# A hand-written end for the last three batches and a reordered start in a cross-attention kernel

## The chip, the cores and the metric

One core of a Trainium2 chip. The time is device microseconds for one execution of the whole kernel, as the median of several runs; the trace comes from one profiled execution.

## The reference

Sixteen batches (B = 16) of cross attention, with 128 query tokens and 20 heads of 8 channels. The context of a batch has 124 text tokens and 4 image tokens of width 256. The image tokens have projections of their own, and their scores get half the cosine between the attended text and the image token.

```python
q = heads(hidden_states @ W_q)
k_t, v_t = heads(text_ehs @ W_k), heads(text_ehs @ W_v)
probs_t = softmax(q k_t^T * attn_scale)
text_out = probs_t v_t
k_ip, v_ip = heads(ip_ehs @ W_k_ip), heads(ip_ehs @ W_v_ip)
attn_scores = q k_ip^T * attn_scale
qsem = l2norm(probs_t @ text_ehs)
sem = qsem . l2norm(ip_ehs)
probs_ip = softmax(attn_scores + 0.5 * sem) * spatial_mask
out = (text_out + probs_ip v_ip) @ W_out + b_out + residual
```

## The kernel before

Each engine has a program written by hand, ordered by semaphores. All run the same loop of windows, one for each batch, w = -1 to 18: windows -1 to 3 and 14 to 18 are written out, 4 to 13 are a hardware loop of two. A window has five slots g = 0 to 4, one for each group of four heads (G = 5, HG = 4). `has(w, lag, ahead)` says whether window w has work for batch w - lag + ahead.

In the window of batch b, TensorE makes the scores of b's five groups (L706: `score_ps` from `q_stack` and `k_diag`, a block-diagonal K of four heads), turns the probs of the group two slots back (L723), and multiplies those of the group three slots back with `main_rhs` (L746, L748: V, the image columns and the Gram matrix of the context, for the value sums and the squared norm of `qsem`). Between these it prepares batch b + 1: the context's Gram matrix G, V and K into the bank `pa` (L686), Q into `pb` (L758), and the transposes of K and Q for groups 0 to 3 (L765, L775) and group 4 (L713, L714). It also finishes batch b - 3: the turn of `attn_out` (L695) and the output product (L732). A `pa` or `pb` product is K or Q split in two float32r parts, a high part copied by ScalarE (L448, L503) and a low part subtracted by VectorE (L633, L565).

ScalarE does the exponentials (L497), the copies `g_stage` (L444), `probsT` (L466) and `k_stack` (L485). It may overwrite `g_stage` only when its copy into `main_rhs`, ten times over, has landed (semaphore s_grep). VectorE does the row maxima (L628), the norms (L608, L610, called a group of norms below), the statistics `guard`, `rden`, `clamped` (L552 to L556) and small steps of the image softmax. GpSimd does the rest of that: a power for `rnorm` (L415, L429), `fused`, `centred`, `ip_probs`, `text`, and `ip_output` (L248 to L256), which weighs the image values (`vrep`) with `ip_probs`. In windows 16 to 18 `ip_output` is VectorE's.

SyncE issues every DMA, in the order of its program. In a window: `k_split` rows of the image tokens from `kip_d`, the context and x of batch b + 2, later xn and `vrep`, then four copies `k_stack` to `k_diag` (L314), `main_rhs` from `g_stage` (L319), four more `k_diag` copies (L324), and the output of b - 3. `kip_d` and `vip_d` are DRAM tensors that the prologue writes with the image projections of all batches. The scores of batch b + 1 wait for its `k_diag` copies (s_kd03, s_kd4), the transposes of K for it wait for its `k_split` load (s_kip_in).

## Time and profile before

| what | us |
|---|---|
| median of 3 runs (lowest, highest) | 233.81 (233.21, 235.36) |
| the profiled execution, its own time | 234.08 |
| its span, first to last instruction | 232.0 |
| TensorE, matmul busy | 207.8 (90% of the span) |
| VectorE busy | 190.8 (82%) |
| ScalarE busy | 170.0 (73%) |
| GpSimd busy | 154.4 (67%) |

Busy shares are means over stages with different limits. Mean granted TensorE clock: 0.958 of full speed. In the profile PE is TensorE, DVE VectorE, ACT ScalarE, POOL GpSimd and SPq the queue of SyncE, which issues the DMAs. A float32 matmul shows as two passes, so a product over two halves of a contraction is x4.

### The profile page before, as it was taken

The numbers are of one execution on the slowest core, as the hardware profiler recorded it, in microseconds if no ns is written. First come the engines' busy times: TensorE is split into PE (matmuls) and PEld (weight loads), VectorE is DVE, ScalarE is ACT, GpSimd is POOL, SyncE is SP. The second block draws the span as 40 slices with busy tenths as digits, with TensorE's granted clock in tenths as the row PEclk, the third lists the DMA queues.
The fourth block names the chain that finished last, engine by engine and source line by source line (L and its number), as shares of the span: only waits on it lengthen the run. The fifth ranks groups of instructions, "written<-read, shape, count | busy, mean of one in ns | idle before, by whom it ended". The sixth has DMA issues, their size and how long they took to land.

```text
span 232.0 us, 6889 instructions
## 1 busy us (share of the span) xinstructions
PE 207.8 (90%) x1562; PEld 192.6 (83%) x1562; DVE 190.8 (82%) x1149; ACT 170.0 (73%) x561; POOL 154.4 (67%) x263
## 2 busy tenths in 40 slices
PE   1948989999999999999999999999999999988433
PEld 1647879998898999999999999999999999977222
DVE  5753778796979798998979897989798979998862
ACT  2063978897978798897969797988888888975000
POOL 5611003649596868788796969696969696979650
PEclk9976999999999999999999999999999999999955
DMA  5405433465355545373736353646454553533030
GB/s 150 124 18 154 104 101 66 124 172 142 104 160 143 149 132 163 87 206 82 204 80 186 104 172 99 167 119 158 132 152 144 145 149 106 143 87 85 1 100 14
DMA packets 46348, 28.57 MB, mean 123 GB/s; under 512 B 7897, under 2 KB 43898, under 8 KB 46330
## 3 DMA queue, kind: packets, MB, share of 16 engines
q1 hardware_dynamic: 46330, 28.38, 44.6%
q8 instruction: 6, 0.10, 0.2%
q14 instruction: 12, 0.10, 0.1%
HBM read 11.11 MB, written 1.52 MB: 54 GB/s over the span
## 4 chain that ended last, share of the span: by engine, by line
PE 61%; DMA 9%; DVE 8%; POOL 7%; ACT 6%; issue 4%; SPq 3%; DVEq 0%; POOLq 0%; ACTq 0%
PE main_ps L746 11%; PE main_ps L748 11%; PE probsT_ps L723 10%; PE pa L686 9%; DMA main_rhs<-g_stage 6%; PE score_ps L706 6%; PE pb L732 5%; POOL rnorm L429 3%; PE pb L758 3%; PE pa L765 2%; ACT probs L497 2%; DVE junk L608 2%; PE pa L775 2%; SPq L324 1%; PE pb L695 1%
## 5 line engine op out<-in xcount | busy, mean ns | idle before, releaser
L497 ACT ACTIVATE probs<-score_ps,negmax 128x124 f32<-128x124 f32 x320 | 93.3, 413 | 0.7 <-DVE negmax L628 0.6
L608 DVE CUSTOM_DVE_ANT_0 junk<-main_ps,probs 128x124 f32<-128x124 f32 x320 | 78.0, 281 | 2.3 <-PE main_ps L748 1.5
L746 PE MATMUL main_ps<-main_rhs,probsT 124*128 124x137 f32 x320 | 65.1, 284 | 1.5 <-DVE small L610 1.4
L748 PE MATMUL main_ps<-main_rhs,probsT 124*128 124x137 f32 x320 | 63.3, 279 | 0.0
L429 POOL TENSOR_TENSOR rnorm<-clamped,exponent 128x20 f32<-128x20 f32 (+1 forms) x16 | 54.8, 3427 | 1.1 <-DVE clamped L556 1.1
L628 DVE TENSOR_REDUCE negmax<-score_ps 128x4 f32<-128x496 f32 x80 | 53.1, 664 | 0.0
L466 ACT ACTIVATE probsT<-probsT_ps 124x512 f32<-124x512 f32 x80 | 51.1, 639 | 2.8 <-PE probsT_ps L723 2.0
L746 PEld LDWEIGHTS main_ps<-main_rhs,probsT 124*128 124x128 f32 x320 | 48.9, 190 | 3.5 <-issue 2.6
L748 PEld LDWEIGHTS main_ps<-main_rhs,probsT 124*128 124x128 f32 x320 | 48.7, 188 | 0.0
L723 PE MATMUL probsT_ps<-ident_sb,probs 128*124 128x128 f32 x320 | 48.2, 273 | 0.0
L723 PEld LDWEIGHTS probsT_ps<-ident_sb,probs 128*124 128x124 f32 x320 | 38.4, 139 | 5.2
L706 PE MATMUL score_ps<-k_diag,q_stack 128*128 128x512 f32 x80 | 39.0, 488 | 0.3 <-ACT probs L497 0.3
L627 DVE COPY ip_score<-score_ps 128x16 f32<-128x16 f32 x80 | 13.3, 166 | 21.4 <-PE score_ps L706 21.4
L610 DVE COPY small<-main_ps 128x26 f32<-128x26 f32 x160 | 28.8, 180 | 0.0
L608 DVE DVE_READ_ACCUMULATOR2_ANT norm<- 128x1 f32 x320 | 26.6, 83 | 0.2 <-issue 0.2
L444 ACT ACTIVATE g_stage<-pa 128x128 f32<-128x128 f32 x16 | 4.4, 278 | 26.5 <-PE pa L686 16.4
L686 PE MATMUL pa<-wkv_sb,ctxT_sb 128*128 128x160 f32 x128 | 21.9, 319 | 0.0
L399 POOL TENSOR_TENSOR ip_exp_half<-ip_exp 128x40 f32<-128x40 f32 x16 | 4.0, 253 | 25.7 <-ACT ip_exp L491 25.7
L686 PEld LDWEIGHTS pa<-wkv_sb,ctxT_sb 128*128 128x128 f32 x128 | 19.8, 208 | 0.0
L248 POOL TENSOR_TENSOR ip_prod<-vrep,ip_probs 128x640 f32<-128x640 f32 x13 | 18.3, 1404 | 0.0
L409 POOL TENSOR_TENSOR main_rhs<-v_stage,one 124x80 f32<-124x80 f32 x16 | 5.1, 321 | 18.9 <-PE main_ps L748 8.9
L732 PE MATMUL pb<-wout_sb,oT 96*128 96x160 f32 x64 | 14.2, 349 | 2.9 <-DVE oT L620 2.9
(91 smaller groups left out, 339.2 us busy)
## 6 DMA issues: line engine op xcount, KB each, us to landing
main_rhs<-g_stage SPq DMA_DIRECT2D x16, 660.0 KB, 4.1
vrep<-vip_d SPq DMA_DIRECT2D x16, 320.0 KB, 3.5
k_diag<-k_stack SPq DMA_DIRECT2D x60, 64.0 KB, 2.1
ctxT_sb<-ctxT SPq DMA_DIRECT2D x16, 124.0 KB, 2.6
xT_sb<-xT SPq DMA_DIRECT2D x16, 80.0 KB, 2.0
xn_sb<-xn SPq DMA_DIRECT2D x16, 80.0 KB, 2.0
out<-out_sb SPq DMA_DIRECT2D x16, 80.0 KB, 1.7
k_diag<-k_stack SPq DMA_DIRECT2D x60, 16.0 KB, 2.0
```

The costliest lines, as they stand in the source:

```text
L429: pool.tensor_tensor(rnorm[:, heads], clamped[:, heads], exponent[:, heads], ALU.pow).then_inc(s_rnorm, 1)
L466: act.activation(probsT[tp][:, :, :].rearrange("t h s -> t (h s)"), probsT_ps[tp][0:T, :], ACT.Copy).then_inc(s_probsT, 1)
L497: last = act.activation(probs[p][:, h, :], score_ps[(p * G + g) % 2][:, j * TOK:j * TOK + T], ACT.Exp, bias=negmax[p][:, h:h + 1])
L608: dve.tensor_tensor_reduce(junk[:, 2 * r + a, :], u, probs[wb][:, h, :], 1.0, 0.0, ALU.mult, ALU.add, norm2[wb][:, h:h + 1])
L610: dve.tensor_copy(small[wb][:, PG * gg + r, :], main_ps[r][:, T:T + SMALL]).then_inc(s_norm, 1)
L628: dve.tensor_reduce(negmax[p][:, HG * g:HG * g + HG], sc[:, :, 0:T], AX_X, ALU.max, negate=True).then_inc(s_max, 1)
L686: mm = pe.matmul(pa[:, lo:lo + width], ctxT_sb[n][:, c, :], r, start=(c == 0), stop=(c == EC - 1))
L706: pe.matmul(score_ps[(p * G + g) % 2][:, :], q_stack[p][:, g, :], k_diag[p][:, g, :, :].rearrange("r h t -> r (h t)"), start=True, stop=Tr ...
L723: mm = pe.transpose(probsT_ps[tp][0:T, j * S:(j + 1) * S], probs[tb][:, HG * tg + j, :], ident_sb[:, :])
L732: mm = pe.matmul(pb[:, 0:C], oT[:, c, :], wout_sb[:, c, :], start=(c == 0), stop=(c == 1))
L746: pe.matmul(main_ps[r][:, 0:MAIN], probsT[mp][:, 2 * r, :], blk[:, RW - MAIN:RW], start=True, stop=True)
L748: pe.matmul(main_ps[r][:, MAIN:2 * MAIN], probsT[mp][:, 2 * r + 1, :], blk[:, 0:MAIN], start=True, stop=True).then_inc(s_main, 1)
```

## The change

The windows are now 0 to 15. What was window -1 is written out at the head of each engine's program, and what were windows 16 to 18 at the end.

At the start, the loads go out in the order of need, those of K and Wq from ScalarE's queue. TensorE first does ten products on a zero tile. K of batch 0 and of batch 1 gets its four image rows from a product with `zip_sb`, a tile that is zero but for the image tokens' columns, accumulated into the same bank. The Gram matrix of batch 0 comes after the transposes and the image products; the first score follows, and then batch 1's K, V and G. Wq is scaled by ScalarE. The copies `kip_split`, `vip_sb` and the new `vipT_sb` are made by VectorE in window 0, slot 2, and `kip_d`, `vip_d`, `smask`, `wout` and the new `hmask` are moved by SyncE after `main_rhs0` and before window 0's own DMAs. The memset of `k_diag1` on GpSimd comes after V of batch 0 is in `main_rhs0`.

At the end, the last three batches (13, 14, 15) do without `vrep` and `ip_output`. For each a small matrix `vw_sb` = blockdiag(V_ip) W_out is made (`vspread`, L1077), and the output is the sum of two products, one from the turned text part and one from the turned image probs. Statistics and powers of batch 15 go in three parts of 12, 4 and 4 heads (`PARTED`). Its text, fused scores, centring and masking are VectorE's. The tiles of this part are its own.

Tiles of 96 rows become 80 or 81. The middle windows are the same.

```diff
-PARTED = 3
+PARTED = (0, 3, 4, 5)
+TAIL = 3
+LAST = B - TAIL
...
+            sp.dma_start(ctxT_sb[0][:, :, 0:T], ctxT[0]).then_inc(s_ctx_in[0], 16)
+            sp.wait_ge(s_zip, 1)
+            sp.dma_start(zip_sb[0][:, :, T:TOK], ipT[:, :, 0:NIP]).then_inc(s_zip_in[0], 16)
+            sp.dma_start(xT_sb[0][:, :, :], xT[0]).then_inc(s_xT_in[0], 16)
+            sp.dma_start(ident_sb[:, :], ident).then_inc(s_ident_in, 16)
             sp.dma_start(ip_sb[:, :], ipn).then_inc(s_ipn_in, 16)
-            sp.dma_start(ipT_sb[:, :, :], ipT).then_inc(s_ipw_in, 16)
-            sp.dma_start(wkvip_sb[:, :, :], wkvip).then_inc(s_ipw_in, 16)
...
-            sp.dma_start(wkv_sb[:, :, :], wkv).then_inc(s_wkv_in, 16)
-            sp.dma_start(ctxT_sb[0][:, :, 0:T], ctxT[0]).then_inc(s_ctx_in[0], 16)
-            sp.wait_ge(s_fill, 1)
-            sp.dma_start(wq_sb[0:CH, :, :], wq).then_inc(s_wq_in, 16)
...
+            sp.dma_start(wkv_sb[:, :, 0:C], wkv[:, :, 0:C]).then_inc(s_wv_in, 16)
+            sp.dma_start(ipT_sb[:, :, :], ipT).then_inc(s_ipT_in, 16)
+            sp.dma_start(wkvip_sb[:, :, C:2 * C], wkvip[:, :, C:2 * C]).then_inc(s_wvip_in, 16)
             sp.dma_start(ctxT_sb[1][:, :, 0:T], ctxT[1]).then_inc(s_ctx_in[1], 16)
...
+            sp.wait_ge(s_zip, 3)
+            sp.dma_start(zip_sb[1][:, :, T:TOK], ipT[:, :, NIP:2 * NIP]).then_inc(s_zip_in[1], 16)
+            sp.dma_start(xT_sb[1][:, :, :], xT[1]).then_inc(s_xT_in[1], 16)
+            sp.wait_ge(s_gstage, 1)
+            sp.dma_start(main_rhs[0][:, :, D + 1:D + 1 + NIP + TOK],
+                         g_stage[:, :].unsqueeze(1).broadcast_to([TOK, NPAIR, NIP + TOK])).then_inc(s_grep[0], 16)
             sp.wait_ge(s_kip, 2)
-            sp.dma_start(k_split[T:TOK, :, :, :, :].rearrange("t h c a d -> t (h c a d)").bitcast(F32),
-                         kip_split[0:NIP, :, :, :, :].rearrange("t h c a d -> t (h c a d)")).then_inc(s_kip_in, 16)
             sp.dma_start(kip_d, kip_split[:, :, :, :, :].rearrange("t h c a d -> t (h c a d)")).then_inc(s_kip_out, 16)
...
             sp.dma_start(vip_d, vip_sb[:, :]).then_inc(s_vip_out, 16)
             sp.dma_start(smask_sb[:, :], smask).then_inc(s_const_in, 16)
-            sp.dma_start(wout_sb[0:CH + 1, :, :], wout).then_inc(s_const_in, 16)
-            sp.wait_ge(s_fill, 3)
...
-            sp.wait_ge(s_vip_out, 16)
...
+            pool.wait_ge(s_k0_mm, 1)
+            pool.tensor_copy(ctxT_sb[0][:, :, T:TOK], ipunitT[:, :, 0:NIP]).then_inc(s_ipcol, 1)
+            pool.wait_ge(s_v0, 1)
+            v_columns(0)
             pool.memset(k_diag[1][:, :, :, :].bitcast(F32), 0.0).then_inc(s_zeros[1], 1)
-            pool.wait_ge(s_fill, 3)
...
+            for k in range(3):
+                heads = slice(HG * PARTED[k], HG * PARTED[k + 1])
+                pool.wait_ge(s_tail_stats, 3 * (k + 1))
+                pool.tensor_tensor(tail_rnorm[:, heads], tail_clamped[:, heads], exponent[:, heads],
+                                   ALU.pow).then_inc(s_tail_rnorm, 1)
...
+            act.dma_start(wkv_sb[:, :, C:2 * C], wkv[:, :, C:2 * C]).then_inc(s_wk_in, 16)
+            act.dma_start(wkvip_sb[:, :, 0:C], wkvip[:, :, 0:C]).then_inc(s_wkip_in, 16)
+            act.dma_start(wq_sb[:, :, :], wq).then_inc(s_wq_in, 16)
+            act.wait_ge(s_wq_in, 16)
+            act.activation(wq_scaled[:, :, :], wq_sb[:, :, :], ACT.Copy, scale=SCALE).then_inc(s_wq, 1)
+            act.wait_ge(s_k0_mm, 1)
+            act.activation(k_split[:, :, :, 0, :], doubled(probsT_ps[0][:, 0:C]), ACT.Copy).then_inc(s_khi, 1)
+            act.wait_ge(s_q_mm, 1)
+            act.activation(q_split[:, :, 0, :, :], doubled(probsT_ps[1][:, 0:C]), ACT.Copy).then_inc(s_qhi, 1)
...
+            act.wait_ge(s_qlo, 1)
+            act.activation(v_stage[:, :], probsT_ps[1][0:T, C:2 * C], ACT.Copy).then_inc(s_v0, 1)
+            act.wait_ge(s_ctx_mm, 1)
+            act.activation(g_stage[:, NIP:NIP + TOK], pa[:, 0:TOK], ACT.Copy)
+            act.activation(g_stage[:, 0:NIP], pa[:, T:TOK], ACT.Copy).then_inc(s_gstage, 1)
...
+                    if g == 2 and w == 0:
+                        dve.wait_ge(s_vipT_mm, 1)
+                        kips = doubled(main_ps[0][0:B * NIP, 0:C])
+                        dve.tensor_copy(kip_split[:, :, :, 0, :].bitcast(F32R), kips).then_inc(s_kip, 1)
+                        dve.wait_ge(s_kip, 1)
+                        dve.tensor_tensor(kip_split[:, :, :, 1, :].bitcast(F32R), kips, kip_split[:, :, :, 0, :],
+                                          ALU.subtract).then_inc(s_kip, 1)
+                        dve.tensor_copy(vip_sb[:, :], main_ps[0][0:B * NIP, C:2 * C]).then_inc(s_vip, 1)
+                        dve.tensor_copy(vipT_sb[:, :, :, :].rearrange("p x k m -> p (x k m)"),
+                                        main_ps[0][0:CH, 2 * C:2 * C + 2 * TAIL * NIP]).then_inc(s_vipT, 1)
                     if has_group(w, g, 4):
...
+            norms(B, 0, 0)
+            norms(B, 0, 1)
...
+            stats(1, PARTED[0], PARTED[1], tiles, s_tail_stats, 0)
+            norms(B, 0, 2)
...
+            stats(1, PARTED[1], PARTED[2], tiles, s_tail_stats, 3)
+            dve.wait_ge(s_fuse, 2 * (B - 1))
+            dve.tensor_reduce(ipmax[:, :], fused[:, :, :], AX_X, ALU.max).then_inc(s_ipmax, 1)
+            dve.wait_ge(s_ipmax, B - 1)
+            dve.tensor_tensor(tail_centred[0][:, :, :], fused[:, :, :],
+                              ipmax[:, :].unsqueeze(2).broadcast_to([S, H, NIP]), ALU.subtract).then_inc(s_tail_centred, 1)
+            norms(B, 0, 3)
...
+            stats(1, PARTED[2], PARTED[3], tiles, s_tail_stats, 6)
...
+            text_out(0, text[0], rden)
+            dve.wait_ge(s_tail_stats, 9)
+            text_out(1, tail_text, tail_rden)
...
+            pe.wait_ge(s_warm, 1)
+            for k in range(10):
+                pe.matmul(main_ps[1][:, 0:128], warm[:, :], warm[:, :], start=True, stop=True)
+            pe.wait_ge(s_ctx_in[0], 16)
+            pe.wait_ge(s_zip, 2)
+            pe.wait_ge(s_wk_in, 16)
+            project(probsT_ps[0][:, 0:C], ctxT_sb[0], lambda c: wkv_sb[:, c, C:2 * C], True, False)
+            pe.wait_ge(s_zip_in[0], 16)
+            pe.wait_ge(s_wkip_in, 16)
...
+            pe.wait_ge(s_ipcol, 1)
+            pe.wait_ge(s_kst03, 1)
+            pe.wait_ge(s_kd03[0], 64)
+            project(pa[:, 0:TOK], ctxT_sb[0], lambda c: ctxT_sb[0][:, c, :], True, True).then_inc(s_ctx_mm, 1)
...
+                    if g == 0 and w == 0:
+                        pe.wait_ge(s_ctx_in[1], 16)
+                        pe.wait_ge(s_gstage, 1)
...
+                        project(pa[:, TOK + C:TOK + 2 * C], ctxT_sb[1], lambda c: wkv_sb[:, c, C:2 * C], True, False)
+                        pe.wait_ge(s_zip_in[1], 16)
+                        project(pa[:, TOK + C:TOK + 2 * C], zip_sb[1], lambda c: wkvip_sb[:, c, 0:C], False, True)
+                        project(pa[:, TOK:TOK + C], ctxT_sb[1], lambda c: wkv_sb[:, c, 0:C], True, True).then_inc(s_k1_mm, 1)
+                        pe.wait_ge(s_ipcol, 2)
+                        project(pa[:, 0:TOK], ctxT_sb[1], lambda c: ctxT_sb[1][:, c, :], True, True).then_inc(s_ctx_mm, 1)
...
+            def turn_text(src, bank):
+                for x in range(2):
+                    mm = pe.transpose(bank[0:CH, x * S:(x + 1) * S], src[:, x * CH:(x + 1) * CH], ident_sb[:, :])
+                return mm
+            def turn_probs(src, bank):
+                return pe.transpose(bank[0:H * NIP, 2 * S:3 * S], src[:, :, :].rearrange("s h m -> s (h m)"), ident_sb[:, :])
+            def project_text(k, bank):
+                for x in range(2):
+                    pe.matmul(bank[:, 0:C], tailT[k][:, x, :], wout_sb[:, x, :], start=(x == 0), stop=False)
+            def project_probs(k, bank):
+                return pe.matmul(bank[:, 0:C], tailT[k][0:H * NIP, 2, :], vw_sb[:, k, :], start=False, stop=True)
...
+            for k in range(TAIL):
+                pe.wait_ge(s_vspread, k + 1)
+                for x in range(2):
+                    mm = pe.matmul(pb[0:CH, k * C:(k + 1) * C], vspread[:, k, x, :], wout_sb[0:CH, x, :],
+                                   start=(x == 0), stop=(x == 1))
+            mm.then_inc(s_vw_mm, 1)
...
+            pe.wait_ge(s_tail_text, 1)
+            turn_text(text[0], score_ps[0]).then_inc(s_tail_tr, 1)
+            pe.wait_ge(s_tail_text, 2)
+            turn_text(tail_text, score_ps[1]).then_inc(s_tail_tr, 1)
+            pe.wait_ge(s_tail_T, 1)
+            project_text(0, pa)
+            pe.wait_ge(s_vw, 1)
+            project_probs(0, pa).then_inc(s_tail_mm, 1)
+            pe.wait_ge(s_tail_T, 2)
+            pe.wait_ge(s_tail_probs, 1)
+            turn_probs(tail_probs[0], score_ps[0]).then_inc(s_tail_tr, 1)
+            pe.wait_ge(s_probsT, B * G)
+            project_text(1, probsT_ps[0])
+            pe.wait_ge(s_tail_T, 3)
+            project_text(2, probsT_ps[1])
+            pe.wait_ge(s_tail_T, 4)
+            project_probs(1, probsT_ps[0]).then_inc(s_tail_mm, 1)
+            pe.wait_ge(s_tail_probs, 2)
+            turn_probs(tail_probs[1], score_ps[1]).then_inc(s_tail_tr, 1)
+            pe.wait_ge(s_tail_T, 5)
+            project_probs(2, probsT_ps[1]).then_inc(s_tail_mm, 1)
```

SyncE, from the last constant of the prologue to window 1's first DMA, before; 0 and 1 in the names are the buffers of even and odd batches, `k_diag1` is batch 1's.

```order
L280 DMA wout_sb<-wout 81x320
L319 DMA main_rhs0<-g_stage 128x10x132 [waits s_zeros1,s_kst03,s_vip_out,s_gstage,s_kip_out,s_fill]
L292 DMA k_split<-kip_d 4x640 [waits s_kq4,s_kT,s_st4]
L297 DMA ctxT_sb0<-ctxT 128x2x124 [waits s_ctx_mm]
L299 DMA xT_sb0<-xT 80x256 [waits s_q_mm]
L314 DMA k_diag1<-k_stack 32x4x128 [waits s_kst03]
L314 DMA k_diag1<-k_stack 32x4x128 x3
L319 DMA main_rhs1<-g_stage 128x10x132 [waits s_gstage]
L324 DMA k_diag1<-k_stack 32x128 [waits s_st4]
L324 DMA k_diag1<-k_stack 32x128 x3
L292 DMA k_split<-kip_d 4x640 [waits s_kq4,s_kT]
```

The same place in the changed program, up to the first `k_diag1` copy of group 4.

```order
L329 DMA main_rhs0<-g_stage 128x10x132 [waits s_gstage]
L332 DMA kip_d<-kip_split 64x640 [waits s_kip]
L334 DMA vip_d<-vip_sb 64x160 [waits s_vip]
L335 DMA smask_sb<-smask 128x1
L336 DMA wout_sb<-wout 81x320
L337 DMA hmask_sb<-hmask 80x40
L353 DMA ctxT_sb0<-ctxT 128x2x124 [waits s_ctx_mm,s_zeros1]
L355 DMA xT_sb0<-xT 80x256 [waits s_q_mm]
L373 DMA k_diag1<-k_stack 32x4x128 [waits s_kst03]
L373 DMA k_diag1<-k_stack 32x4x128 x3
L378 DMA main_rhs1<-g_stage 128x10x132 [waits s_gstage]
L383 DMA k_diag1<-k_stack 32x128 [waits s_st4]
```

`main_rhs0` goes ahead of five DMAs that stood before it, and these now stand ahead of window 0's loads and `k_diag1` copies.

TensorE, from the last Q transposes of batch 0 to the score product of group 1, before.

```order
L775 MATMUL main_ps1<-ident_r_sb,q_split 128x128 x3
L713 MATMUL pb<-ident_r_sb,k_split 128x128 [waits s_qlo]
L714 MATMUL pb<-ident_r_sb,q_split 128x128
L686 MATMUL pa<-ctxT_sb1 128x128 [waits s_kst03,s_qst03,s_ipcol,s_ctx_in1]
L686 MATMUL pa<-ctxT_sb1 128x128
L686 MATMUL pa<-wkv_sb,ctxT_sb1 128x160 x4
L706 MATMUL score_ps0<-k_diag0,q_stack0 128x512 [waits s_qst03,s_kd030,s_kst03]
L758 MATMUL pb<-wq_scaled,xT_sb1 128x160 [waits s_st4,s_xT_in1]
L758 MATMUL pb<-wq_scaled,xT_sb1 128x160
L706 MATMUL score_ps1<-k_diag0,q_stack0 128x512
```

TensorE in the changed program, from the end of the image products to batch 1's Q.

```order
L906 MATMUL main_ps0<-ipT_sb,wkvip_sb 80x12 x4
L865 MATMUL pa<-ctxT_sb0 128x128 [waits s_kd030,s_kst03,s_ipcol]
L865 MATMUL pa<-ctxT_sb0 128x128
L984 MATMUL score_ps0<-k_diag0,q_stack0 128x512 [waits s_kd030,s_qst03,s_ipunitT,s_kst03]
L865 MATMUL pa<-wkv_sb,ctxT_sb1 128x160 [waits s_zip,s_gstage,s_ctx_in1]
L865 MATMUL pa<-wkv_sb,ctxT_sb1 128x160
L865 MATMUL pa<-wkvip_sb,zip_sb1 128x160 [waits s_zip_in1]
L865 MATMUL pa<-wkvip_sb,zip_sb1 128x160
L865 MATMUL pa<-wkv_sb,ctxT_sb1 128x160 x2
L865 MATMUL pa<-ctxT_sb1 128x128 [waits s_ipcol]
L865 MATMUL pa<-ctxT_sb1 128x128
L1024 MATMUL pb<-wq_scaled,xT_sb1 128x160 [waits s_st4,s_xT_in1,s_kd40]
```

The first score stands ahead of batch 1's products instead of behind them; the Gram matrix of batch 0 and two products with `zip_sb1` have joined the row.

VectorE, the last ten instructions before, for batches 14 and 15.

```order
L615 TENSOR_REDUCE ipmax<-fused 128x20 [waits s_fuse]
L620 COPY oT<-pb 80x256 [waits s_final_mm,s_oT_tr]
L582 RECIPROCAL rip<-ipsum 128x20 [waits s_ipprobs,s_ipsum]
L594 TENSOR_TENSOR out_sb0<-pb,xn_sb0 128x160 [waits s_store0,s_xn_in0,s_final_mm]
L248 TENSOR_TENSOR ip_prod<-vrep1,ip_probs 128x640 [waits s_ipout,s_ipprobs,s_vrep_in1]
L253 TENSOR_TENSOR ip_half<-ip_prod 128x320 [waits s_ipout]
L256 TENSOR_TENSOR ip_out<-ip_half 128x160 [waits s_attn,s_ipout]
L577 TENSOR_TENSOR attn_out<-ip_out,text1 128x160 [waits s_oT_tr,s_text,s_ipout]
L620 COPY oT<-pb 80x256 [waits s_final_mm,s_oT_tr]
L594 TENSOR_TENSOR out_sb1<-pb,xn_sb1 128x160 [waits s_store1,s_xn_in1,s_final_mm]
```

VectorE in the changed program, the last but one twelve, from the image softmax of batch 14 to its output.

```order
L800 TENSOR_REDUCE tail_sum<-tail_exp0 128x20 [waits s_tail_exp,s_const_in]
L802 RECIPROCAL tail_rip<-tail_sum 128x20 [waits s_tail_chain]
L804 SCALAR_TENSOR_TENSOR tail_probs0<-tail_exp0,smask_sb,tail_rip 128x80 [waits s_tail_chain]
L833 TENSOR_TENSOR tail_fused<-small1,tail_rnorm 128x80 [waits s_tail_rnorm]
L836 TENSOR_TENSOR tail_fused<-tail_fused,ip_score1 128x80 [waits s_fuse]
L838 TENSOR_REDUCE tail_max<-tail_fused 128x20 [waits s_fuse]
L840 TENSOR_TENSOR tail_centred1<-tail_fused,tail_max 128x80 [waits s_ipmax]
L845 TENSOR_TENSOR out_sb1<-pa,xn_sb1 128x160 [waits s_store1,s_xn_in1,s_tail_mm]
L800 TENSOR_REDUCE tail_sum<-tail_exp1 128x20 [waits s_tail_exp]
L802 RECIPROCAL tail_rip<-tail_sum 128x20 [waits s_tail_chain]
L804 SCALAR_TENSOR_TENSOR tail_probs1<-tail_exp1,smask_sb,tail_rip 128x80 [waits s_tail_chain]
L850 TENSOR_TENSOR out_sb0<-probsT_ps0,xn_sb0 128x160 [waits s_store0,s_xn_in0,s_tail_mm]
```

The rounds of `ip_prod`, `ip_half`, `ip_out`, `attn_out` and `oT` are gone; both batches' image softmaxes follow each other, and only the outputs are left behind them.

## Rows read from the trace of the kernel before

**Rows 1.** Timeline of TensorE, score products of group 0, windows 0, 1, 3, 4, 6, 14. Columns: start us, us, engine, line, operation, output and inputs, count.
```profile
19.64 0.83 PE L706 MATMUL score_ps<-k_diag,q_stack 128*128 128x512 f32 x1
...
29.77 0.50 PE L706 MATMUL score_ps<-k_diag,q_stack 128*128 128x512 f32 x1
...
54.16 0.50 PE L706 MATMUL score_ps<-k_diag,q_stack 128*128 128x512 f32 x1
...
67.29 0.50 PE L706 MATMUL score_ps<-k_diag,q_stack 128*128 128x512 f32 x1
...
92.50 0.50 PE L706 MATMUL score_ps<-k_diag,q_stack 128*128 128x512 f32 x1
...
189.04 0.50 PE L706 MATMUL score_ps<-k_diag,q_stack 128*128 128x512 f32 x1
```

**Rows 2.** The chain of waits at the start: start us, us, what.
```profile
16.25 4.67 DMA main_rhs<-g_stage
...
32.19 2.75 DMA k_split<-kip_d
```

**Rows 3.** Timeline of SyncE's queue, and TensorE's K transposes of window 1; brackets: idle before.
```profile
8.93 0.58 SPq L276 DMA_DIRECT2D kip_d<-kip_split  x1
...
23.77 2.70 SPq L314 DMA_DIRECT2D k_diag<-k_stack  x4
26.51 0.66 SPq L319 DMA_DIRECT2D main_rhs<-g_stage  x1
28.63 3.47 SPq L324 DMA_DIRECT2D k_diag<-k_stack  x4
...
35.07 0.64 PE L765 MATMUL pa<-ident_r_sb,k_split 128*128 128x128 f32 x4 [1.09 <-DMA k_split<-kip_d]
```

**Rows 4.** The chain of waits at the end: the last output product and its addition.
```profile
228.07 1.45 PE pb L732 x4
229.55 0.33 DVE out_sb L594
```

**Rows 5.** Timeline of VectorE: the cast in the prologue, and Q's low part in window 0.
```profile
8.38 2.96 DVE L534 CAST ident_r_sb<-ident_sb 128x128 fp32r<-128x128 f32 x1
...
23.24 0.49 DVE L565 TENSOR_TENSOR q_split<-pb,q_split 128x320 fp32r<-128x320 f32 x1 [0.19 <-ACT q_split L503]
```

**Rows 6.** The chain of waits: the twelve passes of G, V and K, prologue and steady windows.
```profile
8.36 3.07 PE pa L686 x12
...
103.33 1.53 PE pa L686 x12
```

**Rows 7.** DMA issues of the first 22 us: KB each, median us to landing.
```profile
wq_sb<-wq SPq DMA_DIRECT2D x1, 100.0 KB, 4.6
```

**Rows 8.** ScalarE's groups, 5 to 20 us, by form: busy us, mean ns, idle before.
```profile
L479 ACT ACTIVATE k_diag<-pa 32x512 fp32r<-32x512 f32 x4 | 2.4, 588 | 0.9 <-PE pa L765 0.8
```

**Rows 9.** Timeline of ScalarE in window 1.
```profile
30.70 0.28 ACT L444 ACTIVATE g_stage<-pa 128x128 f32<-128x128 f32 x1 [0.58 <-DMA main_rhs<-g_stage]
...
35.74 0.60 ACT L485 ACTIVATE k_stack<-pa 128x512 f32<-128x512 f32 x1 [1.86 <-PE pa L765]
```

**Rows 10.** Timeline of VectorE behind the last scores.
```profile
211.79 0.29 DVE L608 CUSTOM_DVE_ANT_0 junk<-main_ps,probs 128x124 f32<-128x124 f32 x1 [0.49 <-PE main_ps L748]
...
213.46 0.22 DVE L552 SCALAR_TENSOR_TENSOR guard<-small 128x12 f32<-128x12 f32 x1 [0.25 <-POOL text L379]
...
217.11 0.28 DVE L608 CUSTOM_DVE_ANT_0 junk<-main_ps,probs 128x124 f32<-128x124 f32 x1
...
218.12 0.41 DVE L620 COPY oT<-pb 80x256 f32<-80x256 f32 x1
```

**Rows 11.** Timeline of GpSimd: the two parts of batch 15's power.
```profile
214.82 2.28 POOL L415 TENSOR_TENSOR rnorm<-clamped,exponent 128x12 f32<-128x12 f32 x1
...
219.39 1.64 POOL L429 TENSOR_TENSOR rnorm<-clamped,exponent 128x8 f32<-128x8 f32 x1
```

**Rows 12.** Windows view, the last 12 us: busy us by engine, granted clock, DMA share, GB/s.
```profile
220.00:232.00 12.00, 4.17 (x12) 2.49 (x12) 5.64 (x14) 0.27 (x1) 3.62 (x9) 0.50 0.21 55
```

557 lines of the change are left out of this document (372 added, 185 removed).

## Prediction

> **What bounds the kernel now.** I read the page first, then the starts of the score products, then the chain of waits at both ends. The score product of group 0 opens each batch's window; its starts [rows 1] cut the run in three: 19.64 us of prologue, windows 1 to 5 at (92.50 - 29.77)/5 = 12.55 us, and windows 6 to 13 at (189.04 - 92.50)/8 = 12.07 us with TensorE in every piece of the chain. That last number is the work of TensorE; the change leaves it alone, so only the two ends can move the time.
>
> At the start the chain is not TensorE's. It runs through the copy of g_stage into main_rhs0 (issued 16.25, landed 20.92), on which ScalarE waits before it may take batch 1's projection and then the first probs, and later through a small k_split load issued only at 32.19, landed 34.94, which releases the K transposes of window 1 at 35.07 [rows 2, 3]. From 35.07 to 50 the chain is TensorE without a gap. So the question for the prologue is not when the first score starts but **when that product at 35.07 starts**. Why the load is issued so late is seen in SyncE's own queue [rows 3]: four k_diag copies from 23.77 to 26.47, main_rhs1 at 26.51, four more k_diag copies from 28.63 that take 3.47 us.
>
> At the end the last score is done at about 209, and from there to 232.0 one engine after another waits for VectorE's and GpSimd's short steps; each of the last batches costs a whole round through VectorE, TensorE, VectorE, TensorE, VectorE, the last one ending 229.55 + 0.33 [rows 4].
>
> **The start, walked through.** Three things are taken away. The 2.96 us cast of ident_r_sb and the scaling of wq beside it, which were stretched while GpSimd cleared k_diag1 [rows 5]: the cast now comes when GpSimd is idle and the scaling is ScalarE's. The image K copy into k_split becomes part of a product. And main_rhs0 no longer waits for kip_d, vip_d and two constants to be written. Against this stand ten warm products and a longer chain of its own. TensorE's speed here is known at two levels: twelve passes took 3.07 us at 8.36 and 1.53 us at 103.33 [rows 6], so 0.256 or 0.128 us a pass. The warm products are 20 passes from about 1.6 (VectorE's first memset): done at 4.2 to 6.7. K0 is 8 passes: slow, done at 8.7; fast, it is the wq load that holds ScalarE (issued about 2.0, landing 4.6 after its issue [rows 7], then the scaling 0.4: 7.0). Copy and subtraction of the split are 0.5 each, and the Q and V products 1.0: the K transposes start at 8.0 to 9.7; I take 8.7. Then transposes 0.7, two k_diag copies on each of two engines at 0.59 each [rows 8] instead of four on one, group 4's copies, the unit image rows, the image products (8 long and 8 short passes, about 1.5), the G product 0.5 and g_stage 0.45, with a hand-over of 0.05 to 0.1 between engines: 5.2 us in all, so main_rhs0 is issued at **13.9**, 2.35 earlier than 16.25. Bounds: 13.2, and 16.2 if TensorE runs at the slow rate all through. First score about 13.8, nearly 6 us before 19.64.
>
> Now what it brings. ScalarE gets past g_stage at 13.9 + 4.67 = 18.6 instead of 20.92. But kip_d now needs two VectorE copies placed in window 0 behind the first three waits on ScalarE (k_split, then probs of group 0, then q_split; the subtraction behind them ended at 23.7, 2.8 us after the landing) and these take 0.5 each (0.49 for the same form of subtraction) [rows 5]: SyncE stands at that wait until 18.6 + 2.8 + 2 x 0.5 = 22.4. Behind it in the same queue stand kip_d, vip_d, smask, wout, hmask, ctxT and xT, seven issues at 0.58 (kip_d's row [rows 3]), 4.1 us, and only then the k_diag copies of window 1: 26.4 instead of 23.77, **2.6 later**. main_rhs1 moves by the same, to 29.1; in the run before, the second four k_diag copies had 1.46 us of slack behind it (27.17 to 28.63), so they and the k_split load behind them start 2.6 - 1.4 = 1.2 later. ScalarE comes to the same: g_stage of window 1 waits for main_rhs1 (30.70 before), now 33.3, and had 1.86 us idle before k_stack [rows 9]; 0.7 to 1.1 late. So the earlier first score is handed back in the queue, and window 1's K transposes start **1.2 us later**, at about 36.3. With main_rhs0 at 13.2 this is 0.5, with 16.2 it is 3.5. On the gain side it is bounded too: TensorE stood idle only 1.09 us before the product at 35.07 [rows 3], so a load landing early gives at most that. VectorE's four new copies in window 0 (1.5 us) delay probs of group 2 by 0.9; ScalarE has that slack, and the queue above is later anyway. GpSimd's memsets and three spreads in window 0 lie in an idle stretch (it does nothing there that window 1 waits for).
>
> The Trainium skill, page DMA: Bandwidth & Descriptors, section Issuing engines are not separate DMA queues, says that transfers started from two engines run on the same 16 DMA engines and that a second issuer saves only issue time. By that rule the second queue is worth three issues, some 1.5 to 2 us of the first loads, and nothing of their landing once the engines are full; no run here shows it yet, and since my walk hangs on the slow products and on the queue in window 0, it leaves the sum as it is.
>
> **The tail, walked through.** Up to the norms of batch 15's group 2, at 211.79 + 1.0 = 212.8, both programs are the same but for three transposes on TensorE, 0.15 us. A group of norms takes 1.01 us (217.11 to 218.12), a short operation 0.22 (the row at 213.46) [rows 10]; three statistics in a row overlap, and I give them 0.4. VectorE after 212.9: statistics 0.4, norms 1.0, statistics and two short ones 0.9, norms 1.0, statistics 0.4, two text products at 0.33: 217.3. GpSimd's powers run beside it, 2.28 for 12 heads and 1.64 for 8 [rows 11], so 0.16 a head and about 1.0 for four: done at 217.6, hidden. Then three short ones for batch 14 (0.7), four for batch 15 (0.9) and an exponential 0.3, out_sb 0.33 beside it, three short ones (0.7), a transpose, ScalarE's copy and one product (1.1), out_sb 0.33, and hand-overs of 0.05 to 0.1, some 14 of them, 0.9: **222.2** where it was 229.88, and 2.1 more to the end of the store, 224.3. What goes: ip_prod, ip_half, ip_out and attn_out three times, and the strictly serial rounds.
> The price unknown is TensorE's clock. The granted clock is 0.50 over the last 12 us before [rows 12], and there one output product took 1.45 us [rows 4]. If it is at half from 217 on, the two late text products (8 passes at 0.256), three image products and the transposes set the end instead of VectorE, about 2.2 us later: 226.5. There is more TensorE work now between 214 and 217 (12 passes for vw), which speaks for the full rate at first; I take 225.0, near the fast end because VectorE's chain is serial and sets it either way until 220. Tail: **7.0 us shorter**, 5.5 to 7.7.
>
> **Sum.** The profiled execution is 234.08 us with a span of 232.0. Span 232.0 + 1.2 - 7.0 = 226.2, execution 228.3; the median of the runs is 0.27 below the profiled one, so 228.0.
>
> **Rivals.** (a) *The queue does not bind.* The k_diag copies' lateness is covered, and window 1's K transposes move up by the 1.1 us that TensorE allows: 233.8 - 1.1 - 7.0 = 225.7; all 2.35 us of the earlier main_rhs0 carried on: 224.5. For it: the four k_diag issues ahead of that load took 3.47 us where the four before took 2.70 [rows 3], so some of the queue's time is waiting for room, which may fall otherwise now; against it: seven issues in order have no way round. (b) *Half clock in the tail*: 4.8 us gained there, 230.2. (c) *A slow prologue*, main_rhs0 at 16.2: 233.8 + 3.5 - 7.0 = 230.3. (d) *Slower than before: the queue never catches up.* Windows 1 to 5 cost 12.55 instead of 12.07 because main_rhs lands late for g_stage. If the later start in the queue keeps this going at the 1.06 us that window 3 lost (54.16 to 67.29 is 13.13 [rows 1]) through the nine windows to 14, it costs 9.5 us: 233.8 + 1.2 + 9.5 - 7.0 = 237.5. It decides from 0.65 us a window. Against it: windows 6 to 13 are free of it, and the TensorE work that ends them is unchanged. (e) *The change does not do what it says*: first score no sooner than 18; that is (c) at its worst.
>
> **How the numbers follow.** Forecast 0.52; (a) 0.20, of it 0.05 at 224.5; (b) 0.13; (c) with (e) 0.11; (d) and the like 0.04. The range leaves out the far ends of (a), and (d): 224.8 to 231.0. Within 1% (2.3 us either way, about what runs of this kernel can tell from no change) needs both a slow prologue and a half-clock tail: 0.09; faster 0.87; slower 0.04.
>
> **What would show it.** Right: first score near 13.8; SyncE idle until about 22, the first k_diag copy of window 1 near 26, the K transposes of window 1 at 35.5 to 37; windows from 6 on at 12.07; last out_sb 13 us or so after the last score where it was 21. Wrong: k_diag copies issued before 24, K transposes of window 1 before 34, windows that differ from 12.07, or a tail in which TensorE, not VectorE, fills the chain.

## The result, and the profile after

The changed kernel takes 225.66 us (median of 4 runs, 225.16 to 226.25), the kernel before on the same chip 234.24 us (4 runs, 233.21 to 235.36): ratio 0.963, 95% interval 0.958 to 0.969. The profiled span is 223.5 us where it was 232.0, the mean granted clock of TensorE 0.992 where it was 0.958.

I read the starts of the score products first, as before [rows 1]: timeline of TensorE, group 0 of windows 0, 1, 3, 4, 6 and 14.

```profile
12.22 0.47 PE L984 MATMUL score_ps<-k_diag,q_stack 128*128 128x512 f32 x1
...
29.00 0.50 PE L984 MATMUL score_ps<-k_diag,q_stack 128*128 128x512 f32 x1 [0.97 <-DMA k_diag<-k_stack]
...
53.97 0.50 PE L984 MATMUL score_ps<-k_diag,q_stack 128*128 128x512 f32 x1
...
67.11 0.50 PE L984 MATMUL score_ps<-k_diag,q_stack 128*128 128x512 f32 x1
...
91.32 0.50 PE L984 MATMUL score_ps<-k_diag,q_stack 128*128 128x512 f32 x1
...
188.40 0.50 PE L984 MATMUL score_ps<-k_diag,q_stack 128*128 128x512 f32 x1
```

The first score comes 7.4 us sooner (12.22 for 19.64), window 1 only 0.8, windows 3 and 4 0.2, window 6 1.2, and all behind it 0.6. Windows 6 to 13 take (188.40 - 91.32)/8 = 12.13 us, before 12.07; the difference is all in window 6, which takes 12.64 us (its neighbours 12.10 and 12.04). What happened to the 7.4 us stands in SyncE's queue and beside it on ScalarE, which answer to [rows 3, 9]: timeline of SyncE, then TensorE's K transposes of window 1; below them ScalarE. The copy of `g_stage` into `main_rhs` is called the ring copy from here on.

```profile
12.87 0.65 SPq L329 DMA_DIRECT2D main_rhs<-g_stage  x1
20.76 0.57 SPq L332 DMA_DIRECT2D kip_d<-kip_split  x1
...
24.83 2.69 SPq L373 DMA_DIRECT2D k_diag<-k_stack  x4
27.57 0.67 SPq L378 DMA_DIRECT2D main_rhs<-g_stage  x1
28.28 3.41 SPq L383 DMA_DIRECT2D k_diag<-k_stack  x4
31.81 0.41 SPq L348 DMA_DIRECT2D k_split<-kip_d  x1
...
34.84 0.65 PE L1031 MATMUL pa<-ident_r_sb,k_split 128*128 128x128 f32 x4
```

```profile
17.09 0.28 ACT L576 ACTIVATE g_stage<-pa 128x128 f32<-128x128 f32 x1 [4.25 <-DMA main_rhs<-g_stage]
...
31.80 0.28 ACT L576 ACTIVATE g_stage<-pa 128x128 f32<-128x128 f32 x1 [5.08 <-DMA main_rhs<-g_stage]
```

The first ring copy goes out at 12.87 instead of 16.25. ScalarE waits 4.25 us for it, since there is one g_stage; VectorE's copies of the image rows (`kip_split`, `vip_sb`, `vipT_sb`) come behind that; SyncE stands until 20.76, works without a gap from there, sends the second ring copy at 27.57 (26.51 before), and ScalarE waits 5.08 us for that one too. The K transposes of window 1 start at 34.84, before at 35.07: 3.4 us are down to 0.2.

The end answers to [rows 4, 11, 12]. The last score product, before and then changed:

```profile
208.56 0.49 PE L706 MATMUL score_ps<-k_diag,q_stack 128*128 128x512 f32 x1
```

```profile
207.91 0.49 PE L984 MATMUL score_ps<-k_diag,q_stack 128*128 128x512 f32 x1
```

Then, from the changed kernel, the timeline of GpSimd's last power, the chain of waits behind it (start us, us, engine, output, line), and the windows view of the last stretches (stretch, its length, busy us of PE, weight loads, DVE, ACT and POOL, then the granted clock, the DMA share and GB/s).

```profile
216.38 1.02 POOL L525 TENSOR_TENSOR tail_rnorm<-tail_clamped,exponent 128x4 f32<-128x4 f32 x1 [0.35 <-DVE tail_clamped L698]
```

```profile
217.57 0.16 DVE tail_fused L833
...
218.30 0.25 DVE tail_centred L840
...
218.58 0.28 ACT tail_exp L644
...
219.46 0.31 DVE tail_probs L804
...
219.82 0.32 PE score_ps L1053
...
220.16 0.28 ACT tailT L625
...
220.49 0.55 PE probsT_ps L1062 x2
...
221.07 0.33 DVE tail_out L853
```

```profile
216.00:220.00 4.00, 3.62 (x26) 2.94 (x24) 3.65 (x17) 1.71 (x5) 1.05 (x2) 1.00 0.06 20
220.00:223.50 3.50, 0.67 (x3) 0.30 (x2) 0.33 (x1) 0.27 (x1) 0.00 (x0) 1.00 0.15 47
```

### The profile page after: what moved, and what is told of

Same layout as the page of the kernel before. It is cut to its first block, busy times and chain, and to the rows that moved or that the text cites. A ratio compares the mean times of both kernels' runs of the same rounds, so it can differ in the third digit from the quotient of the medians.

```text
span 223.5 us, 6984 instructions
## 1 busy us (share of the span) xinstructions
PE 210.6 (94%) x1619; PEld 197.6 (88%) x1619; DVE 183.7 (82%) x1147; ACT 172.7 (77%) x569; POOL 149.3 (67%) x255
## 4 chain that ended last, share of the span: by engine, by line
PE 68%; DVE 9%; DMA 8%; POOL 4%; issue 4%; ACT 3%; SPq 3%; DVEq 0%; POOLq 0%; ACTq 0%
PE main_ps L952 13%; PE main_ps L954 12%; PE probsT_ps L934 11%; DMA main_rhs<-g_stage 8%; PE pa L924 8%; PE score_ps L984 6%; PE pb L1012 4%; DVE junk L713 3%; PE pb L1024 3%; PE pa L1031 2%; PE main_ps L870 2%; PE pa L1039 2%; POOL rnorm L500 2%; SPq L373 1%; PE probsT_ps L865 1%
## 5 line engine op out<-in xcount | busy, mean ns | idle before, releaser
L500 POOL TENSOR_TENSOR rnorm<-clamped,exponent 128x20 f32<-128x20 f32 x15 | 53.2, 3544 | 1.2 <-DVE clamped L698 1.2
L934 PE MATMUL probsT_ps<-ident_sb,probs 128*124 128x128 f32 x320 | 49.0, 276 | 0.0
L934 PEld LDWEIGHTS probsT_ps<-ident_sb,probs 128*124 128x124 f32 x320 | 39.1, 141 | 5.3 <-issue 0.4
L478 POOL TENSOR_TENSOR ip_exp_half<-ip_exp 128x40 f32<-128x40 f32 x14 | 3.5, 252 | 25.1 <-ACT ip_exp L606 25.1
L576 ACT ACTIVATE g_stage<-pa 128x128 f32<-128x128 f32 x15 | 4.2, 278 | 20.5 <-DMA main_rhs<-g_stage 13.5
L924 PE MATMUL pa<-wkv_sb,ctxT_sb 128*128 128x160 f32 x112 | 17.5, 299 | 0.0
L984 PEld LDWEIGHTS score_ps<-k_diag,q_stack 128*128 128x128 f32 x80 | 15.4, 193 | 1.2 <-DMA k_diag<-k_stack 1.2
L600 ACT ACTIVATE k_stack<-pa 128x512 f32<-128x512 f32 x15 | 9.0, 598 | 9.4 <-PE pa L1031 9.3
L924 PEld LDWEIGHTS pa<-wkv_sb,ctxT_sb 128*128 128x128 f32 x112 | 15.7, 190 | 0.0
```

Source lines behind the costliest of these rows:

```text
L500: pool.tensor_tensor(rnorm[:, :], clamped[:, :], exponent[:, :], ALU.pow).then_inc(s_rnorm, 1)
L924: mm = pe.matmul(pa[:, lo:lo + width], ctxT_sb[n][:, c, :], r, start=(c == 0), stop=(c == EC - 1))
L934: mm = pe.transpose(probsT_ps[tp][0:T, j * S:(j + 1) * S], probs[tb][:, HG * tg + j, :], ident_sb[:, :])
L984: pe.matmul(score_ps[(p * G + g) % 2][:, :], q_stack[p][:, g, :], k_diag[p][:, g, :, :].rearrange("r h t -> r (h t)"), start=True, stop=Tr ...
```

## The experiments

Times are medians. The experiments ran in three sets, each on a chip of its own: old_tail, kip_early, consts_first and no_warm (the kernel before took 234.34 us there); gs2, kip_gs2, kip_fill and one_part (234.42); gs2_consts, after_fill, kip_gs2_fill and best2 (234.63).
**The new prologue alone** (old_tail). The tail's code of all engines is taken back:

```diff
-            for w in range(B - 2, B):
+            for w in range(B - 2, B + 3):
...
-            norms(B, 0, 0)
-            norms(B, 0, 1)
...
```

> The new prologue with the tail of the kernel before (windows B to B+2 for every engine, statistics in two parts, image output on VectorE, no vspread, no vw). Theory, the start's gain is handed back in window 0 and only the tail saves: start and middle as in the changed kernel (last group's scores at 207.9, 0.65 us ahead of the kernel before), tail as before (21.3 us from the last score to the end instead of 13.5), so 225.7 + 7.8 = 233.5 us, 0.7 below the kernel before (0.997). Rival, the prologue alone is worth the 3.4 us by which its first ring copy is issued earlier, and the written-out tail hides that: 230.8 us (0.985). Second rival, the 0.65 us in the middle is of the tail's code in window 0 or of chance: 234.2 us (1.000).

Measured: 234.63 us, ratio 1.002, interval 0.998 to 1.006 (10 runs). That is 1.1 above the theory's 233.5 and nearest to the second rival's 234.2. The prologue alone is worth nothing that can be measured; the tail is worth 234.63 - 225.66 = 9.0 us by the medians.
```profile
36.00:38.00 2.00, 2.00 (x10) 1.84 (x10) 1.51 (x12) 1.97 (x7) 0.00 (x0) 0.50 0.00 1
...
220.00:234.00 14.00, 5.45 (x16) 3.37 (x16) 6.61 (x20) 0.27 (x1) 4.89 (x11) 0.51 0.16 47
```

**The image row copies earlier** (kip_early).

```diff
-                    if g == 2 and w == 0:
+                    if g == 0 and w == 0:
                         dve.wait_ge(s_vipT_mm, 1)
                         kips = doubled(main_ps[0][0:B * NIP, 0:C])
...
```

(The block also stands behind the first scores' maxima now, ahead of the wait for ScalarE's k_split.)

> The changed kernel with VectorE's four copies of the image rows (kip_split in two passes, vip_sb, vipT_sb) made between its first two uses of the scores, at group 0 of window 0, instead of at group 2, so that they run at about 13.5 to 15 us, in VectorE's idle 4.4 us, and SyncE's kip_d, vip_d, three constants, ctxT and xT are issued by about 18.5 instead of 24.8. Theory, SyncE's queue in window 0 hands the start's gain back: the k_diag copies of window 1 at 20 to 20.5 (k_stack is ready at 19.97), its ring copy main_rhs at 22.8 to 23.2 instead of 27.57, its K transposes at 30.5 to 32.5 instead of 35.09, and 221.4 to 223.2 us in all, 2.5 to 4.3 below the changed kernel (225.66). Rival, another chain of window 1 (the projections, GpSimd's v columns, the clock of TensorE) is just as late: transposes at 34 to 35, 225.0 to 225.7 us.

Measured: 222.68 us, 3.0 below the changed kernel, transposes at 32.39: the theory. The gain stands at the transposes (2.45 us) and grows little behind them (2.62 at the last score). SyncE's timeline:

```profile
14.86 0.56 SPq L332 DMA_DIRECT2D kip_d<-kip_split  x1
...
20.71 2.97 SPq L373 DMA_DIRECT2D k_diag<-k_stack  x4
23.73 0.68 SPq L378 DMA_DIRECT2D main_rhs<-g_stage  x1
```

SyncE now waits for k_stack (ScalarE ends it at 20.69), not the other way round.

**Only the constants earlier** (consts_first).

```diff
             sp.dma_start(xT_sb[1][:, :, :], xT[1]).then_inc(s_xT_in[1], 16)
+            sp.dma_start(smask_sb[:, :], smask).then_inc(s_const_in, 16)
+            sp.dma_start(wout_sb[:, :, :], wout).then_inc(s_const_in, 16)
+            sp.dma_start(hmask_sb[:, :, :], hmask).then_inc(s_hmask_in, 16)
```

(The same three lines are gone from behind `vip_d`.)

> The changed kernel with three SyncE DMAs alone moved: smask, wout and hmask are issued right behind xT of batch 1, while SyncE has nothing to do, instead of behind vip_d; they took 22.02 to 23.54 us there. Theory, SyncE's queue in window 0 is the path: everything behind them 1.3 to 1.5 us earlier (k_diag copies of window 1 at 23.4, main_rhs at 26.1), 224.2 to 224.4 us. Rival, the queue is not the path: 225.7 us. A loss would come only from the three loads delaying wvip, ctxT or main_rhs of window 0 in the DMA rings: up to 1 us later first ring copy, 225.7 to 226.7.

```profile
30.00:32.00 2.00, 0.66 (x5) 0.36 (x3) 0.76 (x4) 1.66 (x7) 0.00 (x0) 1.00 0.10 26
32.00:34.00 2.00, 1.55 (x8) 1.58 (x9) 2.00 (x14) 1.52 (x5) 0.00 (x0) 0.66 0.45 109
34.00:36.00 2.00, 2.00 (x10) 1.82 (x10) 1.23 (x12) 0.79 (x3) 0.00 (x0) 0.50 0.00 0
```

My rival here (the queue is not the path, 225.7) came nearer in time than the theory and is wrong by the rows. The 226.48 also lies in the range that I gave for a loss, but its reason, a later first ring copy, did not happen (12.90 for 12.87). The 0.5 us by which the profiled execution ends behind the changed kernel's come in window 6 (13.24 us for 12.64, see gs2 below). The four runs have mean clocks of 0.984 to 0.988, those of the changed kernel 0.983 to 0.992.

**Two g_stage buffers** (gs2).

```diff
-        g_stage = sb("g_stage", [TOK, NIP + TOK])
+        g_stage = two(sb, "g_stage", [TOK, NIP + TOK])
...
-                        wait(act, s_grep[p], 16 * (i + 1))
+                        wait(act, s_grep[n], 16 * (i + p))
```

> The changed kernel with two g_stage buffers instead of one (ScalarE writes g_stage[n] for batch b+1 and waits only for the ring copy of batch b-1 out of it), nothing else. In the changed kernel ScalarE stands idle 4.25 us at 12.85 to 17.09 and 5.08 us before 31.80, both times for main_rhs's copy out of the one g_stage. [...] Rival, SyncE's queue alone is the path, and it is full by itself: 225.0 to 225.7. A loss is possible only if the k_split copies sooner delay the first probs: below 0.5 us.

Measured: 222.01 us, 3.7 below the changed kernel. ScalarE takes batch 1's projection as soon as TensorE has it; kip_d goes out at 19.62 (a microsecond later than I expected, with probs and q_split of window 0 still ahead of it), the transposes start at 32.60, and the clock is 1.00 throughout:

```profile
15.95 0.28 ACT L576 ACTIVATE g_stage<-pa 128x128 f32<-128x128 f32 x1 [3.02 <-PE pa L865]
```

Only 2.2 us of the 3.7 are there at the transposes. The other 1.5 come in later windows, where the one g_stage costs too. ScalarE in the changed kernel, windows 3 and 6:

```profile
55.32 0.28 ACT L576 ACTIVATE g_stage<-pa 128x128 f32<-128x128 f32 x1 [1.29 <-DMA main_rhs<-g_stage]
...
92.24 0.28 ACT L576 ACTIVATE g_stage<-pa 128x128 f32<-128x128 f32 x1 [1.38 <-DMA main_rhs<-g_stage]
```

These windows take 13.14 and 12.64 us there; in gs2, where ScalarE no longer waits for a ring copy, 12.20 and 12.11. The kernel before has the same waits in windows 3, 4 and 5 (1.29, 1.24 and 1.37 us; the windows 13.13, 12.52 and 12.69).

**Both** (kip_gs2: the two diffs together).

> Both together: VectorE's four image row copies at group 0 of window 0 (kip_early, measured 222.68) and two g_stage buffers. [...] Rival, with kip_early done the g_stage wait has slack of its own and only the clock spell moves: 221.5 to 222.7. From 211 us of TensorE work no less than 216 is to be had.

Measured: 219.15 us, transposes at 31.00. The single gains are 2.98 and 3.65, together 6.51: nearly the sum, as it must be where two waits lie behind each other on one path; that the second g_stage also shortens later windows adds to it. Runs at 218.2 and 218.3 (mean clock 0.996, 0.999) and at 220.0 and 220.2 (0.992).

**The constants again, behind two buffers** (gs2_consts).

> gs2 with smask, wout and hmask issued behind xT of batch 1. By itself that move brought SyncE's queue forward by 1.43 us (k_diag copies at 23.41) and no time (226.48), because window 1 took 14.88 us instead of 13.29, with TensorE at 1.2 GHz from 33 to 36 us behind an idle 1.8 us in which ScalarE stood at the ring copy out of the one g_stage. Theory, the queue is the path and what took the gain was that wait with the clock behind it: with two g_stage buffers the 1.4 us come through, k_diag copies of window 1 at 22.2 to 22.4 instead of 23.68, 220.5 to 221.0 us. Rival, the three constants are not on the path at all: 221.7 to 222.3 us.

Measured: 221.33 us, 0.7 below gs2, between theory and rival (runs 220.53 to 222.11; gs2 is of another set, 221.70 to 222.27). In its profile the k_diag copies start at 22.54 and the transposes at 31.57, 1.1 and 1.0 sooner than in gs2, though the prologue of this execution was 0.3 later. So most of the queue's gain comes through once ScalarE's wait is gone; by the times alone this would be weak.

**Without the warm products** (no_warm).

```diff
-            pe.wait_ge(s_warm, 1)
-            for k in range(10):
-                pe.matmul(main_ps[1][:, 0:128], warm[:, :], warm[:, :], start=True, stop=True)
```

> [...]
Measured: 231.07 us, 5.4 above the changed kernel, where I expected 0.7 to 1.7 at the most. TensorE, changed kernel first, then no_warm:

```profile
1.06 4.49 PE L870 MATMUL main_ps<-warm 128*128 128x128 f32 x20 [1.06 <-DVE warm L651]
5.39 0.71 PE L865 MATMUL probsT_ps<-wkv_sb,ctxT_sb 128*128 128x160 f32 x4
```

```profile
4.04 1.44 PE L865 MATMUL probsT_ps<-wkv_sb,ctxT_sb 128*128 128x160 f32 x4 [4.04 <-DMA ctxT_sb<-ctxT]
...
16.42 0.77 PE L981 MATMUL score_ps<-k_diag,q_stack 128*128 128x512 f32 x1
...
19.51 1.27 PE L865 MATMUL pa<-wkv_sb,ctxT_sb 128*128 128x160 f32 x4
21.10 0.71 PE L865 MATMUL pa<-ctxT_sb 128*128 128x128 f32 x4 [0.31 <-POOL ctxT_sb L435]
```

The warm products do not only make the first K product fast; they even start it 1.35 us later (5.39 for 4.04). Without them the groups of four take 1.27 instead of 0.71 us until 21 us, the whole prologue: first ring copy at 17.17, transposes at 39.97. That the granted clock shows 1.00 in these stretches is no help; the duration of one shape is the better witness.

**Filling the idle time of TensorE in window 0** (kip_fill and after_fill: the same edit on kip_early and on the changed kernel; kip_gs2_fill: six products on kip_gs2).

```diff
+                    if g == 1 and w == 0:
+                        for k in range(12):
+                            pe.matmul(main_ps[1][:, 0:128], warm[:, :], warm[:, :], start=True, stop=True)
                     if g == 1 and has(w, ahead=1):
                         wait(pe, s_klo, b + 2)
```

> [...]
The loss in after_fill I did not expect: its windows 2 and 3 took 25.9 us together instead of 24.8. ScalarE waited 1.30 and 1.86 us there for the ring copy out of the one g_stage, 0.76 and 1.29 in the changed kernel, 1.1 us in sum. One_part, whose program is the changed kernel's up to the tail, has such a wait of 1.65 in window 2 (12.57 us for 11.68). So this wait differs between executions without any fill, and whether the twelve products have a part in it stays open.

My account of kip_gs2's two pairs falls: kip_gs2_fill has runs at 218.4 to 218.8 and at 219.7 and 219.9, with the clock at 0.998 or more in all. Its profiled run, 219.88, shows another tie: image row loads that land late in windows 3 and 4, which take 12.79 and 13.13 us instead of 12.12 in kip_gs2. The second stands on SyncE behind the store of a result whose issue takes 1.77 us, 0.58 in kip_gs2; the first is issued at 50.31, behind four k_diag copies. TensorE, then SyncE ahead of the second:

```profile
52.37 0.63 PE L1034 MATMUL pa<-ident_r_sb,k_split 128*128 128x128 f32 x4 [0.45 <-DMA k_split<-kip_d]
...
65.56 0.66 PE L1034 MATMUL pa<-ident_r_sb,k_split 128*128 128x128 f32 x4 [0.83 <-DMA k_split<-kip_d]
```

```profile
61.19 1.77 SPq L388 DMA_DIRECT2D out<-out_sb  x1
63.40 0.30 SPq L348 DMA_DIRECT2D k_split<-kip_d  x1
```

**Statistics of the tail in one part** (one_part).

```diff
-            for k in range(3):
-                heads = slice(HG * PARTED[k], HG * PARTED[k + 1])
-                pool.wait_ge(s_tail_stats, 3 * (k + 1))
-                pool.tensor_tensor(tail_rnorm[:, heads], tail_clamped[:, heads], exponent[:, heads],
-                                   ALU.pow).then_inc(s_tail_rnorm, 1)
+            pool.wait_ge(s_tail_stats, 3)
+            pool.tensor_tensor(tail_rnorm[:, :], tail_clamped[:, :], exponent[:, :], ALU.pow).then_inc(s_tail_rnorm, 1)
```

(VectorE's statistics, in one part too, are not shown.)

> The changed kernel with batch 15's statistics and power in one part of 20 heads behind the last norms instead of three parts of 12, 4 and 4 heads: VectorE runs six short statistics fewer (0.8 to 1.0 us less), GpSimd one power of 20 heads, 3.54 us by its row at 207.91. Theory, VectorE's chain sets the tail and the parts hide the powers: the power starts at about 216 and ends at 219.6, tail_fused at 219.7 instead of 217.57, 2.1 us later: 227.4 to 228.2 us, with VectorE idle 2 us ahead of tail_fused. Rival, the tail is bound by TensorE or ScalarE (vw, tailT copies) and the parts are not needed: 225.0 to 226.0.

Measured: 228.98 us, 3.3 above the changed kernel, more than expected; the profile has the wait that was expected. From the last score to `tail_fused` are 11.93 us there and 9.58 in the changed kernel (its timeline has 217.49), 2.35 more; another 0.65 us of that execution was lost ahead of the last score (208.56 for 207.91). GpSimd, then VectorE:

```profile
216.91 3.55 POOL L523 TENSOR_TENSOR tail_rnorm<-tail_clamped,exponent 128x20 f32<-128x20 f32 x1 [3.97 <-DVE tail_clamped L695]
```

```profile
220.49 0.24 DVE L826 TENSOR_TENSOR tail_fused<-small,tail_rnorm 128x80 f32<-128x80 f32 x1 [2.37 <-POOL tail_rnorm L523]
```

VectorE's chain sets the tail, and the three parts hide GpSimd behind it: some 2.4 us by the profile.

**All together** (best2): two buffers, early image row copies and constants, six products in window 0, and

```diff
             pool.memset(oT[:, :, :], 1.0).then_inc(s_fill, 1)
+            pool.memset(k_diag[1][:, :, :, :].bitcast(F32), 0.0).then_inc(s_zeros[1], 1)
```

in place of the same line at 12.20 us.

> kip_gs2_fill with the constants early and k_diag of odd batches cleared by GpSimd right behind its first memsets, at about 1.8 to 4 us, instead of at 12.20 to 14.44, where it kept GpSimd from ctxT's image columns and TensorE's G product idle for 0.31 us. Theory: 0.3 us by the clearing; SyncE is not waited for any longer in window 0 once the image row copies are early (k_diag copies wait for k_stack at 20 us), so the constants bring nothing: 217.6 to 218.2 us. Rival one: GpSimd's memset beside VectorE's own of k_diag at 1.49 to 3.68 stretches both, VectorE's cast of ident_r_sb is late and the K transposes with it: 218.5 to 220. Rival two: the early constants do count, 216.5 to 217.4.

Measured: 219.06 us (218.51 to 219.24), the same as kip_gs2_fill's 218.72 within the runs' spread, 0.9 above the theory's range and in that of rival one. But rival one's reason did not happen: the two memsets side by side took 2.19 and 2.23 us, as each did alone (2.19, 2.24), and batch 0's K transposes started at 7.83 for 8.13. The transposes start 0.3 sooner (28.88 for 29.17) with a first score 0.3 sooner, and TensorE's idle 0.31 us ahead of its G product is still there, so the clearing was not its cause. What keeps its profiled execution (219.00) up is the tie of kip_gs2_fill: windows 3 and 4 take 12.44 and 12.90 us, with TensorE idle 0.61 us for the image row load at 64.69, behind a store whose issue took 1.36 us. No run tries to remove this tie. The simplest good version is kip_gs2: ratio 0.934 to the kernel before, interval 0.927 to 0.942; kip_gs2_fill has 0.934, 0.931 to 0.938.

## Why the prediction came out as it did

The forecast was 228.0 us with 224.8 to 231.0 around it; 225.66 was measured. The mechanism was the one that happened, the sizes of three terms were off, all to the same side. The forecast span was 226.2 us, the profiled one is 223.5: of the 2.7 us between them 1.4 are the start (transposes 1.2 later forecast, 0.2 sooner measured), 0.4 the middle and 0.8 the tail. Of the signs named, the tail came as said (13.5 us, 13 forecast). The first k_diag copy of window 1 at 24.83 and the transposes at 34.84 fell between the signs for right (near 26, 35.5 to 37) and those for wrong (before 24, before 34).

*The start.* Forecast: ring copy at 13.9, first score near 13.8, window 1's transposes 1.2 later. The profile has 12.87, 12.22 and 0.2 sooner. The part "K0 is 8 passes: slow, done at 8.7" was mis-sized: the warm products brought TensorE to its fast rate by 5.4, before the first weights' product, so that batch 0's K transposes started at 7.69, ahead of the 8.0 to 9.7 that I allowed. From there to the ring copy are 5.18 us, where the walk had 5.2. In other executions the fast rate came later: in kip_gs2 the first two groups took 1.27 and 1.07 us and the ring copy left at 13.80, just the 13.9 of the walk. The rest of the walk fitted: from ring copy to kip_d I had 22.4 - 13.9 = 8.5 and the profile has 20.76 - 12.87 = 7.9; kip_d to the k_diag copies 4.0 (forecast) and 4.07. And the handing back itself is shown: by itself the prologue brings 234.63 against 234.34 us, which leaves -0.4 to +1.3 us for the term of +1.2; undoing either wait of its path brings 3 us or more. What I had not seen as part of it is ScalarE's wait for the single g_stage, read in [rows 9] only as slack and priced only in (d), behind window 1: it is worth as much as the queue (3.7 and 3.0 us), 2.2 of it ahead of the transposes and the rest in later windows.

The warm products are the only step of the new prologue ahead of the ring copy that a run takes away; what the others bring is not measured.

*The middle.* No gain was forecast; 0.4 us came between the transposes of window 1 and the last score (0.2 sooner, then 0.65). The rows say where. In windows 4 and 5 of the kernel before (12.52 and 12.69 us) ScalarE waited 1.24 and 1.37 us for the ring copy, in the changed kernel only once, 1.38 us in window 6 (12.64): windows 4 to 6 take 37.31 us before and 36.85 changed. Old_tail has the gain too, 174.73 us from the transposes to the last score less the 1.64 that its spell added to window 1, with 173.07 in the changed kernel and 173.49 before. One_part, with the same program up to there, has 173.44. So the 0.4 us may be no more than the difference of two executions.

*The tail.* Forecast 7.0 shorter, 7.8 by the profile, 9.0 by the medians with and without it. The walk at the full rate (222.2 for the last addition's end, counted from the old last score) was the right one: 221.40 with a last score 0.65 sooner. The 0.7 us I put on for a half clock (225.0 for 224.3) did not come, and rival (b) with it: the granted clock is 1.00 to the end. TensorE was busy 3.62 of 4 us from 216 to 220, with vw's products and the text products just before and in that stretch, where it was busy 1.30 before; that this kept the clock is likely, and no run shows it by itself. One_part shows VectorE and GpSimd, not TensorE, to be what the tail is made of. The 9.0 us by the medians are 1.2 more than the 7.8 of the two profiles; old_tail's tail took 22.0 us where it was 21.3, and the rest stays open.

*The rivals.* (a), 225.7 or 224.5, named the measured time, but for a reason that did not happen: the queue did bind. (c), a slow prologue with the ring copy at 16.2 at 230.3 us, is what no_warm made: 17.17 and 231.07. (d), a queue that never catches up, did not come: 12.13 us a window from window 6 on. The loss in window 3 on which (d) was priced was read rightly: it goes with the second buffer (12.20 us in gs2). The warm products were in my sum only as a choice between two starts of one product; they decide all passes up to 21 us, 5.4 us.

*The rule on queues.* The Trainium skill, page DMA: Bandwidth & Descriptors, section Issuing engines are not separate DMA queues, was left out of the sum. No experiment put the loads back on one queue, so nothing here tests it. ScalarE's load of wq lands 3.6 us after its issue, before 4.6 from SyncE [rows 7], but this came with other loads around it (DMA issues: KB each, median us to landing):

```profile
wq_sb<-wq ACTq DMA_DIRECT2D x1, 100.0 KB, 3.6
```

## What to carry to other kernels

A prologue that gets the first product out sooner is worth what the first steady window starts sooner, and nothing else: follow the early product's buffers (who may not overwrite them, and for how long a copy reads them) and every DMA issue in order behind the step that was moved. When an edit shortens a queue as planned and the time stays, look for the next engine's idle time and what clock TensorE comes back with before calling the queue harmless. Look for a single buffer that a long copy reads in every window, not only in the first: its wait comes and goes with the copy's landing. In a tail, cut the rounds between engines (here they were only tested all together with the rest of the new tail, 7.8 to 9.0 us; what `vw_sb` alone brings is not measured), and give the slow engine its work in pieces while the bounding one is still busy.

## What was not expected of the hardware

Idle time of nearly the same length was or was not followed by the half clock. Timeline of TensorE in the changed kernel, and the windows view behind each of the two:

```profile
18.54 0.79 PE L1031 MATMUL pa<-ident_r_sb,k_split 128*128 128x128 f32 x4 [1.92 <-DVE k_split L784]
...
33.92 0.47 PE L952 MATMUL main_ps<-main_rhs,probsT 124*128 124x137 f32 x2 [1.84 <-DVE small L715]
```

```profile
20.00:22.00 2.00, 2.00 (x10) 1.82 (x9) 1.68 (x6) 1.73 (x6) 0.00 (x0) 0.50 0.02 5
...
34.00:36.00 2.00, 2.00 (x17) 1.93 (x18) 2.00 (x14) 1.46 (x4) 0.00 (x0) 1.00 0.34 94
```

In consts_first the same place (1.80 us idle) brought the half clock, and in kip_gs2 it came (0.73, 0.50 and 0.91 from 20 to 26 us) with no idle time in window 0 ahead of it longer than 0.71 us, while gs2 has the same 0.71 us and no spell. So the gain of a shorter wait can be taken by the clock behind it, and a single profile doesn't say how often. The Trainium skill, page TensorE: Matmul & The Clock Gate, section What's actually happening, says that the clock is set by how busy the engine has been of late, at one of two rates; the filled versions agree (1.00 with the idle time filled).

The second: without the warm products TensorE stayed at the slow rate to 21 us, although it was busy 1.6 to 2.0 us of each 2 from 4 us on; with ten products without a gap at the start the fast rate was there by 4.8 us in one execution (gs2_consts), by 5.2 to 6.4 in most, by 7.5 in kip_gs2. The kernel before has no such products either, starts TensorE at 5.11 and had the fast rate by 11.55 (four passes of 160 columns in 0.81 us, behind eight in 2.08). So removing the products is shown to cost 5.4 us here; why the slow rate lasted so long in no_warm is not.
